# A transformer layer on one core: two attention output banks, one bank for queries and keys, value projection biases moved to the output bias, and an order of its own at both ends

## The chip, the core and the metric

The kernel runs on one core of one Trainium2 chip. The core's engines work side by side and meet through semaphores: TensorE (PE, with its weight loads as PEld), VectorE (DVE), ScalarE (ACT), GpSimd (POOL) and SyncE (SP), which issues the transfers. The metric is the device time of one execution in microseconds, less is better.

## What is computed

32 sequences of 256 tokens and 128 features go through attention (16 heads of 64) and a feed-forward part with low-rank experts, each behind a layer norm and with a layer norm on its output before the residual is added:

```python
def _L0_attn_ref(x, W_Q, b_Q, W_K, b_K, W_V, b_V, W_O, b_O):
    Q = jnp.einsum('btd,hkd->bthk', x, W_Q) + b_Q
    K = jnp.einsum('btd,hkd->bthk', x, W_K) + b_K
    V = jnp.einsum('btd,hkd->bthk', x, W_V) + b_V
    scores = jnp.einsum('bqhk,bshk->bhqs', Q, K) / jnp.sqrt(jnp.asarray(d_head, x.dtype))
    attn = jax.nn.softmax(scores, axis=-1)
    out_h = jnp.einsum('bhqs,bshk->bqhk', attn, V)
    return jnp.einsum('bqhk,hdk->bqd', out_h, W_O) + b_O
...
    gate = jax.nn.softmax(xt @ gate_w.T, axis=-1)
    base = xt @ weight.T
    t = jnp.einsum('nh,erh->ner', xt, lora_U)
    lora = jnp.einsum('ne,eor,ner->no', gate, lora_V, t)
    out = base + scaling * lora
...
    x = x + _layernorm(_L0_attn_ref(_layernorm(x, axis=-1), ...), axis=-1)
    x = x + _layernorm(_L0_ffn_ref(_layernorm(x, axis=-1), ...), axis=-1)
```

## The kernel before

One item is one sequence b (0 to 31). Heads are handled two at a time, as pairs p = 0 to 7. Projections, scores and output projection are made of three matmuls each on values split into an upper and a lower half (`_hi`, `_lo`, type fp32r); transpositions and the attention output run on fp32.

An item goes through these steps; each is a function with the engine's name above it in the code:

- `stats_x` (VectorE), `ln_rstd`, `norm_x` (GpSimd): layer norm of x. `transpose_xn` (TensorE), `xt_high` (ScalarE), `xt_low` (VectorE): transposed into `xt_hi` and `xt_lo`, plus one. The kernel adds one to x and takes it back through the weights: at the start each weight is centred so that the bias rides on it (`diagonals` on GpSimd, `weight_means` on TensorE, `fold_means` on VectorE, then `weight_hi` on ScalarE and `weight_lo` on VectorE).
- `project_qk(b,p)` (TensorE, six matmuls of 256 columns), `qk_hi` (ScalarE), `qk_lo` (VectorE).
- `project_v(b,quarter)`, three matmuls of 512 columns, `copy_v` (ScalarE).
- `scores(b,p)`, 24 matmuls of 64 rows, two at a time, into `st_ps[p % 2]`; `row_max(b,p,h)` (VectorE), `exponentials` (ScalarE), `invert_sum` (VectorE), `scale_probs` (GpSimd), for each head h of the pair.
- `transpose_probs(b,p,h)` back into the same bank, four transpositions; `copy_probs_t` (h = 0 ScalarE, h = 1 VectorE).
- `probs_v(b,p)`: attention output, eight matmuls of 64 columns of weights, two pairs to a bank; `attention_hi` (ScalarE) and `attention_lo` (VectorE) for each group of two pairs.
- `output_projection` (24 matmuls), `copy_yt`, `transpose_y`, `stats_y`, `residual_x1`, `transpose_x1`, `copy_x1t`, `project_tg`, `gate_max`, `gate_exponentials`, `apply_gate`, `transpose_u`, `copy_ut`, `project_z`, `copy_z`, `stats_z`, `norm_z`: the rest, all through the one bank `extra_ps`. The result is written over the item's x and sent out.

Each engine has its own list of these calls, written out by hand in `body(i)`, which serves three items at once: the first half of item i, the second half of i - 1, the feed-forward part of i - 2. The lists set the order; nothing is reordered on the way. `run` unrolls `body` for i = 0, 1, 2, loops over i = 3 to 31 (29 passes), and unrolls it twice more; in the unrolled ones `live` drops the calls of items that don't exist.

The eight banks of the matmul results are four for scores (`st_ps`), two for queries and keys (`qk_ps`, by p % 2), one for attention output (`o_ps`) and `extra_ps`. A call's `free=` names the semaphore that says that the bank's last content has been read.

Of the kernel before, what the change touches and what calls it, by code (L numbers as in the profile page):

```python
# [13 lines left out]
P = 128  # L14
# [11 lines left out]


# [8 lines left out]


def live(i, lag):

    return not isinstance(i, int) or 0 <= i - lag < B  # L40


def latest(i, *uses):

    for lag, sem, count in uses:
        if live(i, lag):
            return sem, count
    return uses[0][1], 0
# [6 lines left out]
def transformer_layer(nc, x, w_q, w_k, w_v, w_o, biases, ffn_w, out):  # L55
    ctx = ExitStack()
    with ctx:
# [21 lines left out]
        one = sb("one", [P, 1])  # L79
        w_o_mean = sb("w_o_mean", [P, PAIRS])  # L80
# [37 lines left out]
        qk_ps = [bank(f"qk_ps{n}") for n in range(2)]  # L118
        o_ps = bank("o_ps")
# [12 lines left out]
        diag_ready = {n: sem(f"diag_ready_{n}") for n in "qkv"}  # L132
# [9 lines left out]
        ffn_means_projected = sem("ffn_means_projected")  # L142
        w_hi_ready = {n: sem(f"w_hi_ready_{n}") for n in "qkvo"}
# [58 lines left out]
        def x_tile(b, j):  # L202
# [9 lines left out]
            ("v", slice(0, 512), st_ps[1][0], slice(0, 512)),  # L212
            ("v", slice(512, 1024), st_ps[1][1], slice(0, 512)),
            ("q", slice(256, 512), o_ps, slice(0, 256)),
            ("q", slice(512, 1024), st_ps[0][0], slice(0, 512)),
            ("k", slice(256, 512), st_ps[1][0], slice(0, 256)),
            ("k", slice(512, 1024), st_ps[0][1], slice(0, 512)),
# [3 lines left out]
        diag_home = {"v": 1, "q": 2, "k": 3}  # L221
# [45 lines left out]
        def _(pe):  # L267
            def transpose_tiles(dst, src):
# [4 lines left out]
            def weight_means(n, cols, bank, dst):  # L273

                nc.tensor.matmul(bank[:, dst], mean_w[:, :], diag(n, cols),
# [4 lines left out]
            def transpose_xn(b, free):  # L280
                after(pe, *free)
                pe.wait_ge(xn_ready, b + 1)
                transpose_tiles(extra_ps, xn).then_inc(x_transposed, 1)
                if first(b):
                    for n in "qk":
                        pe.wait_ge(diag_ready[n], 1)
                        pe.wait_ge(early_loaded[n], 16)
                    for piece in MEANS[0:2]:
                        weight_means(*piece)

            def project_qk(b, p, free):
# [8 lines left out]
                after(pe, *free)  # L300
# [7 lines left out]
                if first(b) and p == 0:  # L308
                    pe.wait_ge(diag_ready["v"], 2)
                    pe.wait_ge(w_loaded["v"], 16)  # L310
                    for piece in MEANS[2:4]:
                        weight_means(*piece)
                if first(b) and p == 1:
                    pe.wait_ge(mean_folded, 4)
                    for n, pieces in (("q", MEANS[4:6]), ("k", MEANS[6:8])):
                        pe.wait_ge(diag_ready[n], 3)
                        pe.wait_ge(w_loaded[n], 16)
                        for piece in pieces:
                            weight_means(*piece)
                if first(b) and p == 3:  # L320
                    pe.wait_ge(mean_folded, len(MEANS))
                    pe.wait_ge(ffn_rows_centred, 1)
# [800 lines left out]
```

## Time and profile before

| | |
|---|---|
| Median of three runs | 1220.18 us (1218.62 to 1221.35) |
| Profiled execution | 1221.85 us, span 1220.0 us |
| Mean granted TensorE clock | 0.990 |
| TensorE busy | 1185.9 us (97%) |
| ScalarE busy | 967.9 us (79%) |
| VectorE busy | 958.6 us (79%) |
| GpSimd busy | 728.3 us (60%) |

The span runs from the first to the last instruction; the profiled execution took 1.85 us more than its span. Busy is the time in which an engine has an instruction under way. For TensorE the ends of matmuls are modelled and overlap, so its pace is read from the distance between starts.

### The profile page before, as it was taken

Reading aid. Unit: us, or ns where it says so; the run is one execution under the profiler, and the core shown is the slowest. Engines: PE = TensorE matmul, PEld = TensorE weight load, DVE = VectorE, ACT = ScalarE, POOL = GpSimd, SP = SyncE. Lnnn points to the kernel's source line nnn. Section 1 sums busy time; section 2 is a strip of 40 time slices with the busy share of each in tenths; the row PEclk is TensorE's granted clock in tenths of the full one; section 3 lists DMA queues with packets and bytes.
Section 4 is the critical chain, followed back from the end, with each engine's and each line's share of the span. In section 5 each row is a group of like instructions: output and inputs, shape, how many; then the busy total and the mean of one; then the engine's idle time right before and its main releaser. Section 6 shows DMA issues by size and latency. Waiting matters only on the chain.

```text
span 1220.0 us, 32981 instructions
## 1 busy us (share of the span) xinstructions
PE 1185.9 (97%) x10532; PEld 977.1 (80%) x10532; DVE 958.6 (79%) x2618; ACT 967.9 (79%) x3079; POOL 728.3 (60%) x946
## 2 busy tenths in 40 slices
PE   6899999999999999999999999999999999999995
PEld 3688888888888888888888888888888888888883
DVE  4677888887888887887877878877888878788883
ACT  2678888888888888888888888888888888888882
POOL 2556556665556665566665666675556665555653
PEclk9899999999999999999999999999999999999997
DMA  6000000000000000000000000000000000000000
GB/s 213 2 1 6 2 6 4 4 4 4 0 4 4 4 4 4 0 4 4 4 4 4 4 0 4 4 4 4 4 0 4 4 4 4 4 0 4 4 4 9
DMA packets 9923, 10.95 MB, mean 9 GB/s; under 512 B 816, under 2 KB 9392, under 8 KB 9904
## 3 DMA queue, kind: packets, MB, share of 16 engines
q1 hardware_dynamic: 9904, 10.70, 2.7%
q8 instruction: 11, 0.18, 0.1%
q14 instruction: 8, 0.07, 0.0%
HBM read 6.50 MB, written 4.19 MB: 9 GB/s over the span
## 4 chain that ended last, share of the span: by engine, by line
PE 82%; POOL 7%; DVE 6%; issue 4%; ACT 1%; POOLq 0%; DVEq 0%; DMA 0%; SPq 0%; ACTq 0%
PE o_ps L383 17%; PE st_ps L365 17%; PE st_ps L355 14%; PE extra_ps L398 8%; PE qk_ps L304 4%; PE qk_ps L306 4%; PE qk_ps L305 4%; POOL probs L1021 3%; PE extra_ps L337 3%; PE extra_ps L339 2%; PE extra_ps L338 2%; DVE probs_t L806 2%; PE extra_ps L270 2%; POOL xn L1010 1%; POOL xn L1015 1%
## 5 line engine op out<-in xcount | busy, mean ns | idle before, releaser
L1021 POOL TENSOR_TENSOR probs<-probs,inv_sum 128x512 f32<-128x512 f32 x512 | 525.4, 1042 | 352.6 <-DVE inv_sum L801 342.0
L563 ACT ACTIVATE probs<-st_ps,neg_max 128x256 f32<-128x256 f32 x1024 | 475.2, 482 | 102.6 <-DVE neg_max L794 99.7
L794 DVE TENSOR_REDUCE neg_max<-st_ps 128x2 f32<-128x512 f32 x512 | 332.0, 680 | 48.8 <-PE st_ps L355 45.7
L365 PE MATMUL st_ps<-ident,probs 128*128 128x128 f32 x2048 | 286.6, 275 | 6.7 <-POOL probs L1021 5.1
L365 PEld LDWEIGHTS st_ps<-ident,probs 128*128 128x128 f32 x2048 | 233.9, 141 | 46.9 <-POOL probs L1021 21.6
L383 PE MATMUL o_ps<-probs_t,v_sb 128*64 128x256 f32 x2048 | 256.3, 387 | 0.3 <-DVE o_lo L812 0.2
L563 ACT ACTIVATION_READ_ACCUMULATOR probs<-st_ps,neg_max 128x1 f32 x1024 | 217.1, 212 | 0.0
L806 DVE COPY probs_t<-st_ps 128x512 f32<-128x512 f32 x256 | 169.4, 683 | 37.4 <-PE st_ps L365 37.3
L383 PEld LDWEIGHTS o_ps<-probs_t,v_sb 128*64 128x64 f32 x2048 | 133.4, 136 | 73.2 <-issue 5.9
L778 DVE TENSOR_TENSOR qk_lo<-qk_ps,qk_hi 128x512 fp32r<-128x512 f32 x256 | 175.1, 684 | 11.8 <-ACT qk_hi L550 11.5
L571 ACT COPY probs_t<-st_ps 128x512 f32<-128x512 f32 x256 | 152.5, 596 | 32.6 <-PE st_ps L365 32.6
L550 ACT CAST qk_hi<-qk_ps 128x512 fp32r<-128x512 f32 x256 | 152.6, 596 | 17.7 <-PE qk_ps L306 13.8
L355 PE MATMUL st_ps<-qk_hi 64*128 64x256 f32 x1024 | 165.2, 316 | 0.2 <-DVE probs_t L806 0.2
L801 DVE RECIPROCAL inv_sum<-row_sum 128x2 f32<-128x2 f32 x512 | 80.3, 162 | 92.5 <-ACT probs L563 84.1
L355 PE MATMUL st_ps<-qk_lo,qk_hi 64*128 64x256 f32 x1024 | 146.7, 279 | 0.0
L355 PE MATMUL st_ps<-qk_hi,qk_lo 64*128 64x256 f32 x1024 | 145.9, 277 | 0.0
L355 PEld LDWEIGHTS st_ps<-qk_hi 64*128 64x128 f32 x1024 | 98.6, 185 | 24.6 <-issue 17.0
L355 PEld LDWEIGHTS st_ps<-qk_lo,qk_hi 64*128 64x128 f32 x1024 | 99.6, 187 | 0.0
L355 PEld LDWEIGHTS st_ps<-qk_hi,qk_lo 64*128 64x128 f32 x1024 | 99.2, 186 | 0.0
L583 ACT COPY v_sb<-extra_ps 128x512 f32<-128x512 f32 x128 | 76.0, 594 | 29.0 <-PE extra_ps L339 29.0
L304 PE MATMUL qk_ps<-xt_hi,wq_hi 128*128 128x256 f32 x256 | 92.4, 361 | 4.5 <-issue 2.5
L989 POOL TENSOR_TENSOR rstd<-var_eps,neg_half 128x2 f32<-128x2 f32 x128 | 88.8, 694 | 10.0
(116 smaller groups left out, 2073.4 us busy)
## 6 DMA issues: line engine op xcount, KB each, us to landing
out<-x_all SPq DMA_DIRECT2D x32, 128.0 KB, 1.7
x_all<-in_x SPq DMA_DIRECT2D x1, 3840.0 KB, 17.3
stage_v<-in_w_v SPq DMA_DIRECT2D x1, 512.0 KB, 4.1
stage_o<-in_w_o SPq DMA_DIRECT2D x1, 512.0 KB, 6.7
stage_q<-in_w_q SPq DMA_DIRECT2D x1, 384.0 KB, 4.7
stage_k<-in_w_k SPq DMA_DIRECT2D x1, 384.0 KB, 5.8
x_all<-in_x SPq DMA_DIRECT2D x2, 128.0 KB, 3.1
ffn<-in_ffn_w SPq DMA_DIRECT2D x1, 196.0 KB, 6.8
```

The lines of the kernel that those rows point to most:

```text
L304: nc.tensor.matmul(dst, w_hi[w][:, cols], xt_hi[:, :], start=True, stop=False)
L355: last = nc.tensor.matmul(st_ps[p % 2][h][:, j * T:(j + 1) * T], tile(q, j)[head_rows(h), :], k[head_rows(h), :], start=(t == 0), stop=(t ...
L365: last = nc.tensor.transpose(st_ps[p % 2][h][:, s * T + j * P:s * T + (j + 1) * P], probs[p % N_PROBS][h][:, j, s * P:(s + 1) * P], ident[ ...
L383: last = nc.tensor.matmul(o_ps[head_rows(h), cols], v_sb[:, s, p * P + h * DH:p * P + (h + 1) * DH], probs_t[p % N_PROBS_T][h][:, s, :], s ...
L398: last = nc.tensor.matmul(extra_ps[:, 0:T], w["o"][:, cols], o[:, pair, :], start=(pair == 0 and n == 0), stop=(pair == PAIRS - 1 and n == 2))
L550: nc.scalar.copy(qk_hi_sb[p % N_QK][:, :], qk_ps[p % 2][:, :]).then_inc(qk_hi_ready, 1)
L563: last = nc.scalar.activation(probs[n][h][:, j, :], st_ps[p % 2][h][:, j * T:(j + 1) * T], ACT.Exp, bias=neg_max[n][h][:, j:j + 1], accum_ ...
L571: nc.scalar.copy(probs_t[p % N_PROBS_T][0][:, :, :].rearrange("p s q -> p (s q)"), st_ps[p % 2][0][:, :]).then_inc(probs_t_copied[0], 1)
L778: nc.vector.tensor_tensor(qk_lo_sb[n][:, :], qk_ps[p % 2][:, :], f32(qk_hi_sb[n][:, :]), ALU.subtract).then_inc(qk_lo_ready, 1)
L794: nc.vector.tensor_reduce(neg_max[p % N_PROBS][h][:, :], st_ps[p % 2][h][:, :].rearrange("p (j s) -> p j s", j=NT), AX.X, ALU.max, negate= ...
L806: nc.vector.tensor_copy(probs_t[p % N_PROBS_T][1][:, :, :].rearrange("p s q -> p (s q)"), st_ps[p % 2][1][:, :]).then_inc(probs_t_copied[1 ...
L1021: nc.gpsimd.tensor_tensor(probs[n][h][:, :, :], probs[n][h][:, :, :], inv_sum[n][h][:, :].unsqueeze(2).to_broadcast([P, NT, T]), ALU.mult) ...
```

## The change

Five things change.

1. **Banks.** `o_ps` becomes two banks, chosen by the group (`p // 2 % 2`). The output projection goes into `o_ps[1]` instead of `extra_ps`. In exchange `qk_ps` becomes one bank, so that each `project_qk` waits for the `qk_lo` of the pair before it (before: of the pair two before).
2. **Values.** The value weights are no longer centred and biased. The softmax weights of a row sum to one, so what is left out is a constant; it is computed once (`ffn_means`, `centre_ffn_columns`) and added to the output bias (`output_bias`, `centre_output_bias`).
3. **Order in the loop.** All five lists are new. Attention output of pairs 0 to 3 stands in a row, each pair's scores stand alone.
4. **Order at the ends.** Items 0 to 2 and what follows item 31 have lists of their own, written out call by call, instead of `body` with dropped calls.
5. **Warm-up.** Twelve 128-column matmuls on constants stand first on TensorE, and ScalarE's first instruction is a copy of `one`.

```diff
+WARM_UPS = 12
...
-        qk_ps = [bank(f"qk_ps{n}") for n in range(2)]
-        o_ps = bank("o_ps")
+        qk_ps = bank("qk_ps")
+        o_ps = [bank(f"o_ps{n}") for n in range(2)]
...
-            for i in range(lag + 1):
-                body(i)
             with engine.Fori(0, B - 1 - lag) as step:
                 body(step + (lag + 1))
-            for i in range(B, B + lag):
-                body(i)
...
+            def warm_up():
+
+                for _ in range(WARM_UPS):
+                    nc.tensor.matmul(st_ps[1][1][:, 0:P], mean_w[:, :], mean_w[:, :], start=True, stop=True)
...
+            def output_bias():
+
+                pe.wait_ge(v_offset_ready, 1)
+                pe.wait_ge(ffn_ready, 1)
+                pe.wait_ge(w_o_centred, 1)
+                dst = o_ps[1][:, D + TG + PAIRS:D + TG + PAIRS + 1]
+                nc.tensor.matmul(dst, neg_mean_w[:, :], bias[:, B_O:B_O + 1], start=True, stop=False)
+                for pair in range(PAIRS):
+                    last = nc.tensor.matmul(dst, stage["o"][:, pair_cols(pair)], v_offset[:, pair:pair + 1],
+                                            start=False, stop=(pair == PAIRS - 1))
+                last.then_inc(bias_o_projected, 1)
...
-                    dst = qk_ps[p % 2][:, n * T:(n + 1) * T]
+                    dst = qk_ps[:, n * T:(n + 1) * T]
...
+            weight_means(3)
+            project_qk(0, 0)
+            weight_means(4)
+            project_v(0, 1, free=(v_copied[0], 1))
+            weight_means(5)
+            project_qk(0, 1, free=(qk_lo_ready, 1))
+            ffn_means()
+            project_v(0, 2, free=(v_copied[1], 1))
+            scores(0, 0)
+            scores(0, 1)
+            project_qk(0, 2, free=(qk_lo_ready, 2))
+            output_bias()
...
+                scores(i, 4, free0=(probs_t_copied[0], PAIRS * i + 3), free1=(probs_t_copied[1], PAIRS * i + 3))
+                transpose_y(i - 1, free=(v_copied[3], i + 1))
+                project_qk(i, 6, free=(qk_lo_ready, PAIRS * i + 6))
+                scores(i, 5, free0=(probs_t_copied[0], PAIRS * i + 4), free1=(probs_t_copied[1], PAIRS * i + 4))
+                probs_v(i, 0, free=(o_lo_ready, GROUPS * i - 1))
+                probs_v(i, 1)
+                probs_v(i, 2, free=(yt_ready, i))
+                probs_v(i, 3)
+                project_qk(i, 7, free=(qk_lo_ready, PAIRS * i + 7))
+                transpose_x1(i - 1, free=(x1_ready, i))
+                transpose_probs(i, 4, 1, free=(exp_ready[1], PAIRS * i + 5))
+                transpose_probs(i, 4, 0, free=(exp_ready[0], PAIRS * i + 5))
+                transpose_probs(i, 5, 1, free=(exp_ready[1], PAIRS * i + 6))
```

**The loop, scores of pairs 4 and 5 on TensorE.** Before, the two pairs' scores follow one another and attention output of pair 1 follows them (`st_ps` are scores, `o_ps` is attention output, `yt` is the transposition of the output, `qk_ps` a projection):

```order
L270 MATMUL extra_ps<-ident,yt 128x128 x2
L343 REGISTER_ALU
L355 MATMUL st_ps<-qk_hi 128x256 x2
...
L355 MATMUL st_ps<-qk_hi,qk_lo 128x256 x2
L343 REGISTER_ALU
L355 MATMUL st_ps<-qk_hi 128x256 x2
...
L355 MATMUL st_ps<-qk_hi,qk_lo 128x256 x2
L383 MATMUL o_ps<-probs_t,v_sb 64x256 x4
L304 MATMUL qk_ps<-xt_hi,wq_hi 128x256
```

The same place of the changed kernel:

```order
L370 MATMUL st_ps<-ident,probs 128x128 x4
L360 MATMUL st_ps<-qk_hi 128x256 x2
...
L360 MATMUL st_ps<-qk_hi,qk_lo 128x256 x2
L263 MATMUL extra_ps<-ident,yt 128x128 x2
L259 REGISTER_ALU
L326 MATMUL qk_ps<-xt_hi,wq_hi 128x256
...
L328 MATMUL qk_ps<-xt_hi,wk_lo 128x256
L360 MATMUL st_ps<-qk_hi 128x256 x2
...
L360 MATMUL st_ps<-qk_hi,qk_lo 128x256 x2
L259 REGISTER_ALU
L387 MATMUL o_ps<-probs_t,v_sb 64x256 x16
```

The transposition of yt and projection 6 have moved between the two pairs' scores, and the attention output behind them is of four pairs.

**The loop, attention output of pairs 6 and 7.** On TensorE of the changed kernel the scores of item i's pair 0, the last transpositions of item i - 1, projection 2 and the attention output follow one another:

```order
L360 MATMUL st_ps<-qk_hi,qk_lo 128x256 x2
L370 MATMUL st_ps<-ident,probs 128x128 x4
L259 REGISTER_ALU
L326 MATMUL qk_ps<-xt_hi,wq_hi 128x256
...
L328 MATMUL qk_ps<-xt_hi,wk_lo 128x256
L259 REGISTER_ALU
L387 MATMUL o_ps<-probs_t,v_sb 64x256 x8
L360 MATMUL st_ps<-qk_hi 128x256 x2
```

Before, the scores of pair 0 were followed by the transposition of u, transpositions of probabilities, projection 3, `project_z`, the scores of pair 1, and then this attention output. VectorE of the changed kernel has at that place, with the maximum of pair 0 (`neg_max`) ahead of the copy of pair 7 (`probs_t`):

```order
L1084 TENSOR_REDUCE gate_max_raw<-extra_ps 128x2
L1089 TENSOR_TENSOR gate_neg_max<-gate_max_raw,rstd 128x2
L1035 REGISTER_ALU
L1037 TENSOR_TENSOR qk_lo<-qk_ps,qk_hi 128x512
L1042 TENSOR_REDUCE neg_max<-st_ps 128x2
L1054 COPY probs_t<-st_ps 128x512
L1042 TENSOR_REDUCE neg_max<-st_ps 128x2
```

Before, one maximum of pair 0 stood ahead of that copy as well, but with more of TensorE's work between.

**The start, VectorE.** Before, from the fold of the last early piece to the first maximum:

```order
L704 TENSOR_TENSOR stage_k<-stage_k,st_ps 128x512
L694 SCALAR_TENSOR_TENSOR wq_lo<-stage_q,wq_hi 128x768
L778 TENSOR_TENSOR qk_lo<-qk_ps,qk_hi 128x512
L694 SCALAR_TENSOR_TENSOR wk_lo<-stage_k,wk_hi 128x768
L746 TENSOR_REDUCE w_o_mean<-stage_o 128x8
L749 TENSOR_SCALAR w_o_mean<-w_o_mean 128x8
L794 TENSOR_REDUCE neg_max<-st_ps 128x2
```

After, from the statistics of item 2 (`stats_x(2)`, the rows that read `x_all`) on:

```order
L967 BN_STATS stats<-x_all 128x6 x2
L970 COPY stats_seen<-stats 128x1
L972 BN_AGGR mean_var<-stats 128x2 x2
L961 TENSOR_TENSOR stage_k<-stage_k,o_ps 128x256
L1037 TENSOR_TENSOR qk_lo<-qk_ps,qk_hi 128x512
L952 SCALAR_TENSOR_TENSOR wq_lo<-stage_q,wq_hi 128x768
L952 SCALAR_TENSOR_TENSOR wo_lo<-stage_o,wo_hi 128x1024
L961 TENSOR_TENSOR stage_k<-stage_k,st_ps 128x512
L1037 TENSOR_TENSOR qk_lo<-qk_ps,qk_hi 128x512
L1022 TENSOR_TENSOR v_offset<-bias,o_ps 128x8
L1025 TENSOR_TENSOR ffn<-ffn,o_ps 128x264
L952 SCALAR_TENSOR_TENSOR wk_lo<-stage_k,wk_hi 128x768
```

The statistics of items 1 and 2 have moved ahead of the first `qk_lo`, and the set-up of the output weights and the feed-forward weights ahead of the first maximum, which is the next instruction. Items 2 to 31 come in one transfer, the last that SyncE issues before its loop.

## Rows read from the trace of the kernel before

**Rows 1.** The page, its groups by cost: busy us, mean ns of one

```profile
PE 1185.9 (97%) x10532; PEld 977.1 (80%) x10532; DVE 958.6 (79%) x2618; ACT 967.9 (79%) x3079; POOL 728.3 (60%) x946
...
L806 DVE COPY probs_t<-st_ps 128x512 f32<-128x512 f32 x256 | 169.4, 683 | 37.4 <-PE st_ps L365 37.3
```

**Rows 2.** Windows: stretch, its us, busy us (instructions) by engine

```profile
core 0: us, PE busy (x) PEld busy (x) DVE busy (x) ACT busy (x) POOL busy (x), PEclk, DMA share, GB/s
...
20.00:30.00 10.00, 7.46 (x29) 4.70 (x28) 7.55 (x12) 4.17 (x6) 0.00 (x0) 1.00 0.20 64
30.00:40.00 10.00, 7.83 (x55) 6.32 (x55) 6.39 (x18) 7.39 (x22) 5.03 (x4) 0.83 0.01 2
40.00:50.00 10.00, 7.02 (x54) 5.11 (x54) 6.53 (x19) 5.34 (x20) 4.99 (x5) 0.92 0.00 1
...
600.00:700.00 100.00, 99.86 (x903) 82.24 (x901) 81.64 (x220) 83.51 (x268) 60.57 (x78) 1.00 0.01 3
```

**Rows 3.** The tile xn on TensorE, whole span, and 91 to 94 us

```profile
L270 PE MATMUL extra_ps<-ident,xn x64: 272/273/445, 7.5 to 1147.5; 128*128 128x128 f32 x64
...
L270 PE MATMUL extra_ps<-ident,xn x2: 272/272/273, 92.5 to 92.6; 128*128 128x128 f32 x2
```

**Rows 4.** TensorE's timeline, 679 to 690 us: start, us, what

```profile
679.82 0.28 PE L306 MATMUL qk_ps<-xt_hi,wk_lo 128*128 128x256 f32 x1
680.03 0.39 PE L355 MATMUL st_ps<-qk_hi 64*128 64x256 f32 x2
680.25 0.28 PE L355 MATMUL st_ps<-qk_lo,qk_hi 64*128 64x256 f32 x2
680.37 0.28 PE L355 MATMUL st_ps<-qk_hi,qk_lo 64*128 64x256 f32 x2
...
683.53 0.50 PE L337 MATMUL extra_ps<-wv_hi,xt_hi 128*128 128x512 f32 x1
683.87 0.39 PE L338 MATMUL extra_ps<-wv_lo,xt_hi 128*128 128x512 f32 x1
684.10 0.40 PE L339 MATMUL extra_ps<-wv_hi,xt_lo 128*128 128x512 f32 x1
...
688.32 0.60 PE L365 MATMUL st_ps<-ident,probs 128*128 128x128 f32 x4
688.68 0.36 PE L304 MATMUL qk_ps<-xt_hi,wq_hi 128*128 128x256 f32 x1
...
689.47 0.38 PE L433 MATMUL extra_ps<-ffn,x1t 128*128 128x128 f32 x2
```

**Rows 5.** Timelines of TensorE and GpSimd, 709 to 711 us

```profile
709.18 3.20 POOL L1021 TENSOR_TENSOR probs<-probs,inv_sum 128x512 f32<-128x512 f32 x3
...
709.95 0.28 PE L306 MATMUL qk_ps<-xt_hi,wk_lo 128*128 128x256 f32 x1
...
710.28 0.66 PE L365 MATMUL st_ps<-ident,probs 128*128 128x128 f32 x4
```

**Rows 6.** Timeline of all engines, 26 to 39 us

```profile
26.30 0.95 DVE L694 SCALAR_TENSOR_TENSOR wq_lo<-stage_q,wq_hi 128x768 fp32r<-128x768 f32 x1
...
31.10 0.28 PE L355 MATMUL st_ps<-qk_hi,qk_lo 64*128 64x256 f32 x2
...
31.42 0.69 DVE L794 TENSOR_REDUCE neg_max<-st_ps 128x2 f32<-128x512 f32 x1 [1.38 <-PE st_ps L355]
...
38.27 1.84 PE L365 MATMUL st_ps<-ident,probs 128*128 128x128 f32 x12 [0.40 <-POOL probs L1021]
```

**Rows 7.** SyncE's timeline at 5 us, and transfers: KB, us to landing

```profile
5.61 0.61 SPq L259 DMA_DIRECT2D x_all<-in_x  x1
...
x_all<-in_x SPq DMA_DIRECT2D x1, 3840.0 KB, 17.3
```

**Rows 8.** Timeline of all engines, 1198 to 1200 us

```profile
1198.75 0.39 PE L398 MATMUL extra_ps<-o_hi,wo_hi 128*128 128x256 f32 x1
1198.87 0.59 ACT L576 CAST o_hi<-o_ps 128x512 fp32r<-128x512 f32 x1 [1.51 <-PE o_ps L383]
...
1199.49 0.69 DVE L812 TENSOR_TENSOR o_lo<-o_ps,o_hi 128x512 fp32r<-128x512 f32 x1 [1.27 <-ACT o_hi L576]
```

More of the change, by code:

```diff
@@ new lines, in _ @@
+            invert_sum(0, 0, 1)
+            invert_sum(0, 1, 0)
+            invert_sum(0, 1, 1)
+            copy_probs_t(0, 0)
+            qk_lo(0, 3)
+            row_max(0, 2, 0)
+            row_max(0, 2, 1)
+            copy_probs_t(0, 1)
+            invert_sum(0, 2, 0)
+            qk_lo(0, 4)
+            stats_x(3)
+            invert_sum(0, 2, 1)
+            attention_lo(0, 0)
+            row_max(0, 3, 1)
+            row_max(0, 3, 0)
+            qk_lo(0, 5)
+            copy_probs_t(0, 2)
@@ new lines, in _ @@
+            invert_sum(0, 3, 1)
+            invert_sum(0, 3, 0)
+            qk_lo(0, 6)
+            row_max(0, 4, 0)
+            copy_probs_t(0, 3)
+            row_max(0, 4, 1)
+            invert_sum(0, 4, 0)
+            invert_sum(0, 4, 1)
+            row_max(0, 5, 1)
+            row_max(0, 5, 0)
+            qk_lo(0, 7)
+            xt_low(1)
+            copy_probs_t(0, 4)
+            invert_sum(0, 5, 1)
+            invert_sum(0, 5, 0)
+            attention_lo(0, 1)
+            qk_lo(1, 0)
@@ new lines, in _ @@
+            invert_sum(1, 0, 1)
+            qk_lo(1, 3)
+            attention_lo(0, 3)
+            row_max(1, 1, 0)
+            row_max(1, 1, 1)
+            copy_probs_t(1, 0)
+            invert_sum(1, 1, 0)
+            invert_sum(1, 1, 1)
+            qk_lo(1, 4)
+            copy_probs_t(1, 1)
+            qk_lo(1, 5)
+            row_max(1, 2, 0)
+            row_max(1, 2, 1)
+            row_max(1, 3, 1)
+            invert_sum(1, 2, 0)
+            row_max(1, 3, 0)
+            stats_y(0)
@@ new lines, in _ @@
+            invert_sum(1, 2, 1)
+            invert_sum(1, 3, 1)
+            residual_x1(0)
+            invert_sum(1, 3, 0)
+            stats_x1(0)
+            qk_lo(1, 6)
+            copy_probs_t(1, 2)
+            copy_probs_t(1, 3)
+            copy_x1t(0)
+            attention_lo(1, 0)
+            qk_lo(1, 7)
+            row_max(1, 4, 0)
+            row_max(1, 4, 1)
+            row_max(1, 5, 1)
+            invert_sum(1, 4, 0)
+            row_max(1, 5, 0)
+            xt_low(2)
+            invert_sum(1, 4, 1)
@@ new lines, in _ @@
+            stats_z(0)
+            qk_lo(2, 5)
+            row_max(2, 2, 0)
+            row_max(2, 2, 1)
+            row_max(2, 3, 1)
+            invert_sum(2, 2, 0)
+            row_max(2, 3, 0)
+            invert_sum(2, 2, 1)
+            invert_sum(2, 3, 1)
+            invert_sum(2, 3, 0)
+            copy_probs_t(2, 2)
+            copy_probs_t(2, 3)
+            stats_y(1)
+            row_max(2, 4, 0)
+            row_max(2, 4, 1)
+            qk_lo(2, 6)
+            invert_sum(2, 4, 0)
@@ new lines, in _ @@
+            residual_x1(1)
+            attention_lo(2, 0)
+            row_max(2, 5, 1)
+            row_max(2, 5, 0)
+            invert_sum(2, 4, 1)
+            stats_x1(1)
+            invert_sum(2, 5, 1)
+            copy_x1t(1)
+            qk_lo(2, 7)
+            invert_sum(2, 5, 0)
+            copy_probs_t(2, 4)
+            attention_lo(2, 1)
+            copy_probs_t(2, 5)
+            xt_low(3)
+            row_max(2, 6, 0)
+            row_max(2, 6, 1)
+            row_max(2, 7, 0)
@@ new lines, in _ @@
+            invert_sum(2, 6, 0)
+            row_max(2, 7, 1)
+            invert_sum(2, 6, 1)
+            qk_lo(3, 0)
+            gate_max(1)
+            invert_sum(2, 7, 0)
+            invert_sum(2, 7, 1)
+            copy_probs_t(2, 6)
+            qk_lo(3, 1)
+            row_max(3, 0, 0)
+            copy_probs_t(2, 7)
+            apply_gate(1)
+            row_max(3, 0, 1)
+            qk_lo(3, 2)
+            invert_sum(3, 0, 0)
+            row_max(3, 1, 0)
+            invert_sum(3, 0, 1)
```

1203 lines of the change are left out of this document (800 added, 403 removed).

## The prediction

> **What bounds the kernel now.** I read the page's first lines, then the windows, the waits of TensorE, and the timeline of one steady item. TensorE is busy for 97% of the span [rows 1]. In the steady middle it is busy 99.86 of 100 us at the full clock, with VectorE at 82, ScalarE at 84 and GpSimd at 61 [rows 2]. Item starts (the transposition of xn) lie at 92.6 and 1147.5 for items 2 and 31, so one item takes (1147.5 - 92.6) / 29 = 36.38 us [rows 3]. Thirty-two items are 1164 us of 1220; some 56 us lie at the ends. So only two things can move the time: what TensorE needs per item (29 passes of the loop), and the ends. An engine with slack, or a bank that comes free earlier, is worth nothing in the loop unless TensorE waits for it. It waits in one real place: `transpose_probs(i,4,0)` starts 0.33 us after the matmul before it where 0.12 is the pace, on the end of GpSimd's scaling (709.18 plus one third of 3.20 us, against 710.28) [rows 5]. That is 0.21 us per pass, 6 us in all.
>
> **What TensorE pays per item now.** The matmuls of both kernels are the same in number and shape in the loop; only their order and banks change. But the timeline shows that order has a price. TensorE runs three array shapes: 128\*128 (projections, transpositions), 64\*128 (scores), 128\*64 (attention output). Within a shape a start follows the last by 0.12 us (680.25 to 680.37 for a pair of score matmuls). At a change of shape the last of the old takes 0.21 (679.82 to 680.03) and the first of the new 0.22 (680.03 to 680.25), or 0.34 instead of 0.23 for a 512-column one after attention output (683.53, 683.87, 684.10) [rows 4]. So one change of shape costs about 0.09 + 0.10 = 0.19 us. Going from a transposition to a projection costs nothing of the kind (688.32 to 688.68 is 0.36 for four transpositions, to 689.47 is 0.79 for six projection matmuls, together 1.15 for ten) [rows 4].
>
> The Trainium skill says so too, and it speaks against this change: TensorEngine Tiling (Array Packing), section Key Properties, has it that changing the tiling mode, not merely the tile, drains TensorE. It gives no price; the rows above agree with it.
>
> **The loop's order, counted.** I counted stretches of one shape in the order of both kernels. Before, a pass has five stretches of scores (pairs 6 and 7 together, 0, 1, 2 and 3 together, 4 and 5 together), five of attention output, six of the rest: 16 changes. After, all eight scores stand alone, attention output has three stretches (4-5, 6-7, 0 to 3), the rest eight: 19 changes. "Four pairs in a row" saves two stretches and the split scores add three, each with a stretch of the rest beside it. That is 3 x 0.19 = +0.57 us per pass. The wait on GpSimd should go: the two transpositions of pair 4 now stand behind attention output of four pairs (about 3.6 us) and projection 7, while GpSimd's input for it does not come later; -0.21. Net +0.36 per pass, x 29 = **+10.4 us**. Outside the loop the two orders differ by 99 - 87 = 12 further changes, **+2.3 us**.
>
> **One bank for queries and keys.** `project_qk(p+1)` now waits for `qk_lo(p)`. Its path is 0.3 to start (as 31.10 to 31.42) [rows 6], 0.6 on ScalarE, 0.7 on VectorE (as the two copies of a bank at the end) [rows 8]. That is 1.6 us. The narrowest place of the new order is between projections 1 and 2: two sets of transpositions (0.36 each), scores (0.8) and a change of shape on either side, 1.9 us from last matmul to first [rows 4]; between the others lie 2 to 7 us. I walked one pass with these durations and found the answer 0.2 us early there and 0.4 or more elsewhere. I take 0, and up to 0.3 per pass as upper bound. Two attention banks: before, attention output waited nowhere in the loop for its bank, so the second saves nothing there; I take 0, also as a lower bound.
>
> **A new wait.** The hand walk found one. Attention output of pairs 6-7 needs `copy_probs_t(7)` on VectorE, and in VectorE's order `row_max(i,0,0)` stands ahead of that copy. That maximum starts 0.32 us after the last score row (31.10 to 31.42) [rows 6], the next instruction 0.62 later, the copy takes 0.68 [rows 1], hand-over 0.06 (710.22 to 710.28) [rows 5]: 1.68. TensorE has between that score row and the attention output 0.21, one set of transpositions 0.36, projection 2 at 0.79 and 0.09 for leaving the shape: 1.45 [rows 4]. So it waits 0.23; behind it stand scores of pair 1 and all that follows. Before, three blocks lay in that place. Bounds 0 and 0.4; I take 0.2, **+5.8 us**.
>
> **The start.** Now: first maximum at 31.42, first transposition of probabilities at 38.27 [rows 6]; TensorE is busy 7.5, 7.8 and 7.0 us of the stretches 20 to 30, 30 to 40 and 40 to 50, at clocks 1.00, 0.83 and 0.92 [rows 2]. The change drops the folding of means into the value weights (four of the 512-column pieces on TensorE, two on VectorE), brings the table load and the weights' upper halves forward, and warms TensorE up. But VectorE now meets `stats_x(2)` ahead of `qk_lo(0,0)`, and its input is the 3840 KB transfer, issued at 5.61 and landing 17.3 us later, at 22.9 [rows 7]. All of VectorE's work behind it waits, and so does projection 1 on TensorE, which stays idle from about 16 to 25. From 22.9 on stand statistics, folds, `qk_lo` twice, two small centrings, and lower halves of 768, 1024 and 768 columns. The last three are 0.95 for 768 [rows 6] and four thirds of it for 1024, 3.2; the two `qk_lo` 1.4 (as a copy of a bank) [rows 1]; for the rest, eight short operations on smaller tiles, I estimate 3 from the same rate. The first maximum comes at about 30 to 32, no earlier than now by more than 1.5. What follows is better ordered: no set-up of VectorE is left between the first maxima, so the first transposition comes at about 35 and scores of pair 5 some 5 us earlier than now, with attention output further on. I take **-8 us**, bounds -3 (TensorE at half clock after its pause) and -12 (no gap at all behind the first transposition).
>
> **The end.** Output projection now accumulates in the second attention bank, which also holds the last group. Before, 18 of its 24 matmuls ran while that group was still being copied (1198.75 on, ScalarE 1198.87, VectorE 1199.49) [rows 8]; now the first waits for both copies, 1.3 us and hand-overs. Waits of the last pairs shrink a little. **+1 us**, bounds 0 and +2. In the loop the same wait for `o_lo` is covered: transpositions, a value projection, projection 3.
>
> **Sum:** 10.4 + 2.3 + 5.8 - 8 + 1 = +11.5. The profiled execution took 1221.85 (span 1220.0 and 1.85 around it), the median of the runs is 1220.18, 1.67 lower: 1231.7, so 1232.
>
> **The rivals.**
> A, the forecast: changes of shape decide, with the small new wait; 1226 to 1241. Chance 0.52.
> B: no new wait, and a start better than I take: 10.4 + 2.3 - 11 + 1 = +2.7, 1223; range 1218 to 1226. For it speaks that a hand walk rounds against the kernel; against it, VectorE standing until 22.9. Chance 0.19; about half of it is within 0.2%.
> C, the other side: faster, because a change of shape is cheaper where the new stretches are short (scores to projection and attention output to scores hardly occur in the loop now, so no steady row prices them). At half the price a pass has 0.28 - 0.21 = +0.07, 2 us; outside 1.1; with -8 + 1 that is -4, 1216; at no price -13, 1207. It decides below 0.13 us per change (5 us from the ends over 29 passes, plus the 0.21 that goes). Against it: both ends of every change in the steady rows cost 0.09 or more. Chance 0.13.
> D: more waits. ScalarE and VectorE are 82% busy and the walk left 0.4 us at several places (scores of 0, 2, 3); if three of them miss by 0.15, +13 more: 1245. The longest ranges of slack in the order before were longer, since pairs of scores bought time. Chance 0.16.
>
> **Numbers.** 0.2% (2.4 us) is about what a measurement of this kernel can tell from no change. Faster by more than that is C alone and a little of B: 0.14. Within it, most of the lower half of B: 0.09. Slower: 0.77. The range leaves out C and the end of D: 1219 to 1244.
>
> **What would show it.** Right: item period 36.9 to 37.1 between transpositions of xn; 0.2 us at each change of shape, also for scores to projection; no wait of `transpose_probs(4,0)` on GpSimd, and one of about 0.2 before attention output of pair 6 on VectorE's copy; VectorE idle until 22.9 on the x transfer; first transposition of probabilities near 35. Wrong: a period at or below 36.5 (then C), or above 37.3 with waits for `probs_t` or `qk_lo` spread over the pass (D), or a steady state reached 10 us earlier than now (B).

## The result, and the profile after

The changed kernel takes 1236.24 us (median of 4 runs, 1235.91 to 1236.63), the kernel before 1220.13 on the same chip: ratio 1.0133, 95% interval 1.0115 to 1.0150. It is slower, by less than 2%. The forecast was 1232 with a range of 1219 to 1244. The profiled execution has a span of 1234.4 us against 1220.0.

The page's first line and the windows of the kernel after (stretch, its us, busy us of each engine, granted clock) answer to [rows 1, 2]:

```profile
PE 1203.6 (98%) x10580; PEld 999.8 (81%) x10580; DVE 970.8 (79%) x2617; ACT 953.9 (77%) x3080; POOL 724.4 (59%) x944
```

```profile
core 0: us, PE busy (x) PEld busy (x) DVE busy (x) ACT busy (x) POOL busy (x), PEclk, DMA share, GB/s
20.00:30.00 10.00, 6.21 (x27) 5.89 (x27) 5.32 (x13) 1.43 (x2) 0.88 (x2) 0.61 0.15 51
30.00:40.00 10.00, 10.00 (x68) 8.75 (x66) 4.84 (x12) 5.29 (x19) 3.06 (x4) 0.70 0.00 1
40.00:50.00 10.00, 8.97 (x77) 6.84 (x76) 8.30 (x20) 7.50 (x25) 5.66 (x9) 1.00 0.01 2
600.00:700.00 100.00, 100.00 (x900) 82.89 (x899) 82.48 (x229) 80.76 (x263) 63.35 (x84) 1.00 0.01 4
```

TensorE is now busy for all of the middle, and still the kernel is slower: it gets through the same matmuls of a pass more slowly. From 20 to 40 us its granted clock is 0.61 and 0.70, where it was 1.00 and 0.83.

The transpositions of xn on TensorE in the kernel after, over the whole span and near 136 us, answer to [rows 3]:

```profile
L263 PE MATMUL extra_ps<-ident,xn x64: 272/273/328, 7.2 to 1161.6; 128*128 128x128 f32 x64
...
L263 PE MATMUL extra_ps<-ident,xn x2: 273/273/273, 136.2 to 136.3; 128*128 128x128 f32 x2
```

Item 3 is the first whose transposition stands at the same place of the work in both lists. It starts at 136.2 (before 128.8), that of item 31 at 1161.5 (before 1147.3), and the span ends 72.9 us later (before 72.7). So the 14.4 us are +7.4 up to item 3, +6.8 over 28 items (0.24 each, of which the first pass, with 37.58, has 1.2 us alone; behind it a pass takes 36.58 against 36.38), and +0.2 at the end. By then four pairs' attention output "in a row" has done 1.9 us and transpositions another 0.7 that were still to come before; counted in work, the start is some 4.8 and the end some 2.8 longer.

Where the 0.20 us of a steady pass come from shows when TensorE's time is summed by kind (each block from its first start to the first start of the next, my sum over the trace, mean of 27 passes, the first pass of the loop left out):

```
us per pass                         before   after   pair 4   projection  scores pulled
                                                     moved    1 between   forward
scores                               6.75     7.28      6.75       6.94       7.14
attention output                     7.66     7.36      7.66       7.66       7.36
projections of queries and keys      6.58     6.68      6.43       6.60       6.67
gate projection                      0.46     0.57      0.46       0.46       0.57
values, output projection, z         7.06     7.06      7.07       7.08       7.06
all transpositions                   7.87     7.65      7.90       8.51       7.65
sum                                 36.38    36.58     36.26      37.25      36.44
```

(The last three columns are experiments below.) Three more stretches of scores cost 0.53, two fewer of attention output give back 0.30, and the rest falls on the blocks between.

The table leaves half of each change of shape with the neighbouring block. Summed at the changes themselves (the last step from start to start in the old shape and the first in the new, less the pace inside the shape; over 20 passes of the trace), the 16 changes of a pass cost 2.92 us before and the 19 cost 3.58 after. That is 0.18 and 0.19 each, and every kind of change lies between 0.15 and 0.23. So three more changes cost 0.65, and 0.45 went elsewhere. Most of it went at the end of a pass. TensorE there, before (projection 7, transposition of pair 4, jump back, transposition of xn, attention output):

```profile
564.46 0.28 PE L306 MATMUL qk_ps<-xt_hi,wk_lo 128*128 128x256 f32 x1
564.78 0.66 PE L365 MATMUL st_ps<-ident,probs 128*128 128x128 f32 x4
565.34 0.43 PE L270 MATMUL extra_ps<-ident,xn 128*128 128x128 f32 x2
565.70 0.87 PE L383 MATMUL o_ps<-probs_t,v_sb 128*64 128x256 f32 x6
```

and after (twelve transpositions of probabilities, jump back, transposition of xn):

```profile
574.89 1.47 PE L370 MATMUL st_ps<-ident,probs 128*128 128x128 f32 x12
576.20 0.38 PE L263 MATMUL extra_ps<-ident,xn 128*128 128x128 f32 x2
576.42 0.60 PE L370 MATMUL st_ps<-ident,probs 128*128 128x128 f32 x4
```

After, each transposition takes 0.11 (1.31 for twelve, 0.22 for the two of xn). Before, the step to the transposition of pair 4 took 0.32, 0.21 more than the pace, its four took 0.56 instead of 0.44, and the two of xn 0.36, which is 0.05 more than 0.22 and a change's 0.09. These 0.38 us have gone; another 0.08 went at the scores of pair 3 (0.89 before where the second pair of a couple takes 0.81), whose cause I have not looked into.

### The profile page after: what moved, and what is told of

Read it like the earlier page. It is cut to its first block, busy times and chain, and to the rows that moved or that the text cites. A ratio compares the mean times of both kernels' runs of the same rounds, so it can differ in the third digit from the quotient of the medians.

```text
span 1234.4 us, 33065 instructions
## 1 busy us (share of the span) xinstructions
PE 1203.6 (98%) x10580; PEld 999.8 (81%) x10580; DVE 970.8 (79%) x2617; ACT 953.9 (77%) x3080; POOL 724.4 (59%) x944
## 4 chain that ended last, share of the span: by engine, by line
PE 94%; DVE 2%; DMA 1%; POOL 1%; ACT 1%; issue 0%; SPq 0%; POOLq 0%; DVEq 0%; ACTq 0%
PE o_ps L387 19%; PE st_ps L360 19%; PE st_ps L370 18%; PE o_ps L401 8%; PE qk_ps L326 6%; PE qk_ps L328 5%; PE qk_ps L327 5%; PE extra_ps L263 3%; PE extra_ps L340 3%; PE extra_ps L342 2%; PE extra_ps L341 2%; PE extra_ps L423 2%; DMA x_all<-in_x 1%; PE extra_ps L436 1%; PE extra_ps L438 1%; POOL probs L1497 1%
## 5 line engine op out<-in xcount | busy, mean ns | idle before, releaser
L1042 DVE TENSOR_REDUCE neg_max<-st_ps 128x2 f32<-128x512 f32 x512 | 341.1, 681 | 90.6 <-PE st_ps L360 85.8
L387 PE MATMUL o_ps<-probs_t,v_sb 128*64 128x256 f32 x2048 | 244.4, 385 | 0.2 <-ACT probs_t L710 0.2
L702 ACT ACTIVATION_READ_ACCUMULATOR probs<-st_ps,neg_max 128x1 f32 x1024 | 220.5, 215 | 0.0
L387 PEld LDWEIGHTS o_ps<-probs_t,v_sb 128*64 128x64 f32 x2048 | 138.7, 137 | 73.5 <-issue 1.8
L1054 DVE COPY probs_t<-st_ps 128x512 f32<-128x512 f32 x256 | 175.1, 685 | 14.1 <-PE st_ps L370 10.5
L360 PE MATMUL st_ps<-qk_hi 64*128 64x256 f32 x1024 | 171.2, 330 | 1.5 <-ACT probs_t L710 1.3
```

The lines of the kernel that those rows point to most:

```text
L360: last = nc.tensor.matmul(st_ps[p % 2][h][:, j * T:(j + 1) * T], tile(q, j)[head_rows(h), :], k[head_rows(h), :], start=(t == 0), stop=(t ...
L387: last = nc.tensor.matmul(o_ps[p // 2 % 2][head_rows(h), cols], v_sb[:, s, p * P + h * DH:p * P + (h + 1) * DH], probs_t[p % N_PROBS_T][h] ...
L702: last = nc.scalar.activation(probs[n][h][:, j, :], st_ps[p % 2][h][:, j * T:(j + 1) * T], ACT.Exp, bias=neg_max[n][h][:, j:j + 1], accum_ ...
L1042: nc.vector.tensor_reduce(neg_max[p % N_PROBS][h][:, :], st_ps[p % 2][h][:, :].rearrange("p (j s) -> p j s", j=NT), AX.X, ALU.max, negate= ...
L1054: nc.vector.tensor_copy(probs_t[p % N_PROBS_T][1][:, :, :].rearrange("p s q -> p (s q)"), st_ps[p % 2][1][:, :]).then_inc(probs_t_copied[1 ...
```

## The experiments

In the code cuts the arguments are left out. Each ratio is to the kernel before, run on the same chip; chips differ from experiment to experiment.

**A change of shape, by itself.**

```diff
-project_qk(i, 1, ...)
 scores(i - 1, 6, ...)
+project_qk(i, 1, ...)
 scores(i - 1, 7, ...)
```

> The kernel before, with projection 1 of the next item put between the scores of pairs 6 and 7, which stood in a row; nothing else is changed. A pass gets two changes of array shape more, with the same matmuls. If a change of shape costs TensorE 0.19 us wherever it stands, the period grows by 0.38 us and 30 items by some 11 to 12 us (1232 against 1220). If short stretches change shape more cheaply, or the cost is hidden, the time stays within 3 us of before.

1248.58 us, ratio 1.0228 (1.0211 to 1.0244): more than either theory said. TensorE's waits from 150 to 1150 us (waited for: us in total, times, longest), and its timeline at one of them:

```profile
PE st_ps L355 <- DVE probs_t L807: 10.9, 27, 0.4
```

```profile
618.58 1.04 PE L365 MATMUL st_ps<-ident,probs 128*128 128x128 f32 x8
...
620.02 0.39 PE L355 MATMUL st_ps<-qk_hi 64*128 64x256 f32 x2 [0.40 <-DVE probs_t L807]
```

Of 0.87 us more per pass, 0.47 is a new wait (from 618.58 to 620.02 it is 1.44, where eight transpositions and a change take 0.97): scores of pair 6 now come before VectorE has copied the transpositions that stood in their bank; projection 1 had covered that copy. The other 0.40 belong to two changes. The table shows the scores apart at 6.94 instead of 6.75, which is half of it. A change of shape does cost 0.20 here; and a block that is moved also stops covering what it covered.

**The wait on GpSimd, by itself.**

```diff
-transpose_probs(i, 4, 0, ...)        # end of the pass
 ...
 probs_v(i - 1, 3)
+transpose_probs(i - 1, 4, 0, ...)
 transpose_probs(i - 1, 4, 1, ...)
```

> The kernel before, with the first transpositions of pair 4 moved from the end of a pass to the next pass, directly ahead of the second ones. It takes away TensorE's wait for GpSimd's scaling and nothing else; the number of changes of shape is the same. If the wait is worth only what I read (0.21 us), the period falls by 0.2 and the time by 6 us. If the jump back to the head of the loop had been paid for too, because nothing was queued in front of TensorE when it waited, the period falls by 0.33 to 0.38 and the time by 9 to 11. If GpSimd only makes another instruction late instead, it falls by nothing.

1217.80 us, ratio 0.9976 (0.9965 to 0.9988), period 36.26 instead of 36.38. The projections of queries and keys fall by 0.15 and the transpositions of probabilities by another 0.12: 0.27 at a place where I had read 0.21, and the last step before the jump back still takes 0.17 where 0.12 is the pace. But the transposition of xn grows by 0.16, up to a wait of TensorE's weight load (150 to 1150 us):

```profile
PEld o_ps L383 <- DVE o_lo L812: 9.1, 28, 0.3
```

Attention output of pair 2 now meets its one bank before VectorE has read it. The wait on GpSimd had hidden this one. In the changed kernel, with its second bank, there is no such row; its order differs too, so the bank by itself is not shown to be the reason.

**Joining scores again, three ways.** First all four, by pulling projections ahead:

```diff
 transpose_probs(i - 1, 5, 0, ...)
-scores(i - 1, 6, ...)
 project_qk(i, 0, ...)
+scores(i - 1, 6, ...)
 scores(i - 1, 7, ...)
...
-scores(i, 4, ...)
 transpose_y(i - 1, ...)
 project_qk(i, 6, ...)
+scores(i, 4, ...)
 scores(i, 5, ...)
```

> The changed kernel, with scores of pairs 4 and 5 and of pairs 6 and 7 put in a row again in the loop (projection 6 with the transposition of y goes ahead of scores 4, projection 0 ahead of scores 6). A pass has four changes of shape fewer, 15. If they cost 0.19 us each and no wait comes in their place, the period falls by 0.76 us, and the time by 22 us, to some 1214, below the kernel before. If the other engines' order makes TensorE wait for the banks of scores or of queries and keys, part of that is lost: 1220 to 1236. If changes of shape are free, nothing moves.

1298.87 us, ratio 1.0643 (1.0629 to 1.0658). It has four changes of shape fewer and is 5% slower than the change itself. TensorE's waits, 150 to 1150 us:

```profile
PE qk_ps L326 <- DVE xt_lo L992: 21.8, 26, 0.8
PE st_ps L370 <- POOL probs L1497: 6.7, 25, 0.3
PE extra_ps L263 <- ACT v_sb L722: 6.2, 26, 0.2
```

Projection 0 stands right behind the transposition of xn and waits 0.8 for its two halves, and scores that come later make GpSimd's scaling late. These idle times are 1.3 us of the 2.3 by which a pass grew; the rest I have not traced. Then only pairs 4 and 5, on the kernel with the late statistics (below, 1225.31):

```diff
-scores(i, 4, ...)
-transpose_y(i - 1, ...)
 project_qk(i, 6, ...)
+transpose_y(i - 1, ...)
+scores(i, 4, ...)
 scores(i, 5, ...)
```

> The changed kernel with the late statistics (1225.3), and in the loop projection 6 and the transposition of y ahead of the scores of pair 4 instead of behind them: scores of pairs 4 and 5 in a row, 17 changes of shape instead of 19. Between the last quarter of values and the transposition of y stand a set of transpositions and projection 6 (1.15 us), so the wait on the copy of values seen when all four scores were joined should not come. Scores of pair 4 start 1.2 us later; from their end to the transposition of pair 4 there are still 5.5 us. If only changes of shape count: period -0.38, time -11, some 1214. If the chain of pair 4 (maximum, exponentials, scaling) is longer than 5.5 us, its transpositions wait and half or more of it is lost: 1219 to 1226.

1234.30 us, ratio 1.0113 (1.0096 to 1.0130), and 0.26 us more per pass. The timeline of GpSimd and TensorE at the head of the loop:

```profile
602.15 3.04 POOL L1497 TENSOR_TENSOR probs<-probs,inv_sum 128x512 f32<-128x512 f32 x3 [0.40 <-DVE inv_sum L1049]
...
604.80 0.43 PE L263 MATMUL extra_ps<-ident,xn 128*128 128x128 f32 x2
...
605.33 0.65 PE L370 MATMUL st_ps<-ident,probs 128*128 128x128 f32 x4
```

The scaling of pair 5 ends at 605.19, and its transposition starts at 605.33, 0.53 after that of xn where 0.22 is the pace: not pair 4 but the end of the same chain is late. Last, the second of each couple pulled forward, on the same kernel:

```diff
 scores(i, 4, ...)
+scores(i, 5, ...)
 transpose_y(i - 1, ...)
 project_qk(i, 6, ...)
-scores(i, 5, ...)
...
 scores(i - 1, 6, ...)
-project_qk(i, 0, ...)
 scores(i - 1, 7, ...)
+project_qk(i, 0, ...)
```

> The changed kernel with the late statistics (1225.3), with the same two pairs of scores joined as in the run that joined all four, but by pulling the second of each forward (pair 5 directly behind pair 4, pair 7 directly behind pair 6) instead of putting projections ahead of the first. No score comes later than now. A pass has 17 changes of shape, two fewer. If a change costs 0.19 us here too and what spoiled the joined versions was only the lateness of their scores: period -0.38, time -11, some 1214. If the copies of the transpositions just ahead are late for the pulled scores, waits of 0.1 to 0.2 appear there: 1217 to 1221. If changes of shape in this order cost nothing, 1225.

1221.28 us, ratio 1.0000 (0.9990 to 1.0009): 4 us faster than without, not 11. The period falls by 0.14. TensorE and ScalarE where pair 7 follows pair 6:

```profile
601.75 0.58 ACT L710 COPY probs_t<-st_ps 128x512 f32<-128x512 f32 x1
```

```profile
602.26 0.28 PE L360 MATMUL st_ps<-qk_hi,qk_lo 64*128 64x256 f32 x2
602.43 0.38 PE L360 MATMUL st_ps<-qk_hi 64*128 64x256 f32 x2
602.62 0.31 PE L360 MATMUL st_ps<-qk_lo,qk_hi 64*128 64x256 f32 x2
```

Pair 7 starts 0.17 after pair 6's last matmul instead of 0.12, just behind the copy's end (602.33), and the next follows 0.19 later instead of 0.12. So this joined pair gives back 0.12 of its 0.19; over the pass, two changes fewer kept 0.14 us.

**Attention output in a row, in the kernel before.**

```diff
 scores(i, 3, ...)
-probs_v(i, 0, ...)
 output_projection(i - 1, 0, ...)
...
 scores(i, 5, ...)
+probs_v(i, 0, ...)
 probs_v(i, 1)
```

(on the kernel with the transpositions of pair 4 moved, 1217.80)

> The kernel before with the first transpositions of pair 4 moved (1217.8), and attention output of pair 0 moved down beside that of pair 1, behind the scores of pairs 4 and 5. It is one part of the change (attention output in a row) by itself; 15 changes of shape instead of 16, and no other engine's order moves. If a change costs 0.19 us: period -0.19, time -6, some 1212. If attention output of pair 0 had covered a copy that now is waited for, less than half of it.

1238.06 us, ratio 1.0139 (1.0124 to 1.0155). TensorE's waits, 150 to 1150 us:

```profile
PE st_ps L365 <- POOL probs L1021: 9.8, 27, 0.4
```

Attention output falls from 7.66 to 7.51 as it should. But the transpositions of pair 2, which come 1.0 us earlier after their scores, wait for GpSimd: with all that follows the period grows by 0.63, to 36.89. I had looked for a copy that it covered, and the cover was for the softmax chain.

**The statistics at the start.**

```diff
 fold_means(3)
-stats_x(2)
 fold_means(4)
 qk_lo(0, 0)
 ...
 weight_lo("k", late, ...)
+stats_x(2)
 row_max(0, 0, 0)
```

> The changed kernel, with the statistics of the whole x transfer moved on VectorE from ahead of the first lower half of queries and keys to just ahead of the first maximum of scores. VectorE stood idle there from 17.6 to 22.0 us on the transfer. If that wait is what spoiled the start, the first maximum comes 3 to 4.4 us earlier and the time falls by 3 to 5 us. If what follows is set by something else (TensorE at half clock, its one-column matmuls, the waits in the hand-written lists of items 1 and 2), the first maximum may come earlier and the time moves by less than 1.5 us.

1225.31 us, ratio 1.0044 (1.0030 to 1.0058): 10.9 us less, more than twice what I allowed. In the kernel after, VectorE and TensorE wait one for the other, and then:

```profile
22.02 0.49 DVE L967 BATCH_NORM_STATS2 stats<-x_all 128x6 f32<-128x128 f32 x2 [4.45 <-DMA x_all<-in_x]
...
23.81 0.58 PE L326 MATMUL qk_ps<-xt_hi,wq_hi 128*128 128x256 f32 x1 [3.79 <-DVE qk_lo L1037]
...
26.14 3.41 PE L291 MATMUL o_ps<-one,stage_v 128*128 128x1 f32 x16
29.41 0.77 PE L340 MATMUL extra_ps<-wv_hi,xt_hi 128*128 128x512 f32 x1
...
31.35 0.41 PE L360 MATMUL st_ps<-qk_lo,qk_hi 64*128 64x256 f32 x2
31.56 0.41 PE L360 MATMUL st_ps<-qk_hi,qk_lo 64*128 64x256 f32 x2
```

The same blocks with the statistics late:

```profile
18.09 0.39 PE L326 MATMUL qk_ps<-xt_hi,wq_hi 128*128 128x256 f32 x1 [0.21 <-DVE qk_lo L1037]
...
19.34 1.84 PE L291 MATMUL o_ps<-one,stage_v 128*128 128x1 f32 x16
21.05 0.48 PE L340 MATMUL extra_ps<-wv_hi,xt_hi 128*128 128x512 f32 x1
...
22.14 0.28 PE L360 MATMUL st_ps<-qk_lo,qk_hi 64*128 64x256 f32 x2
22.25 0.28 PE L360 MATMUL st_ps<-qk_hi,qk_lo 64*128 64x256 f32 x2
```

After the pause TensorE starts a pair of score matmuls every 0.21 us instead of every 0.12, and this lasts until 35: the lower of its two levels, 1.2 of 2.4 GHz (the granted clock is 0.50 in each 2 us stretch from 24 to 34). In this run item 3 begins at 125.0, 3.8 us before the kernel before, with its 2.6 us more work done.

**The pause filled, the wait kept.**

```diff
 weight_means(5)
+for _ in range(20):
+    nc.tensor.matmul(o_ps[0][:, :], tile(xt_hi, 0), w_hi["v"][:, 0:HALF], start=True, stop=True)
 project_qk(0, 1, ...)
```

> The changed kernel as it was measured, with 20 matmuls more whose result nobody reads (values of item 0 once more, into the free first attention bank), put into TensorE's idle time ahead of the second projection at the start. VectorE's wait for the x transfer stays. If the wait alone made the start slow, the time stays at 1236 or grows a little. If TensorE's pause of 5 us cost a second time, through the half clock that followed it (from 24 to 35 us), the blocks behind it get their full-clock times (4.15 to 2.15 us for the means, 2.86 to 1.62 for the first scores, and four more): 5 to 5.5 us less, some 1231, although TensorE does more.

1230.14 us, ratio 1.0080 (1.0065 to 1.0095): 6.1 us less than the change, with 4.6 us more for TensorE to do. The granted clock is 1.00 from 18 to 40 us, the means take 2.15 us and the first scores 1.62. So of the 11 us that the statistics cost, some 6 are the half clock and some 5 the wait.

**The output bias, and the tail**, both on the kernel with the late statistics:

```diff
-output_bias()
 project_v(0, 3, ...)
 transpose_probs(0, 0, 0, ...)
 project_qk(0, 3, ...)
+output_bias()
```

(VectorE's `centre_output_bias` moves behind three inverses to match.)

> The changed kernel with the late statistics (1225.3), and the nine one-column matmuls of the output bias moved from ahead of the first transposition of probabilities to behind projection 3, where TensorE waited for GpSimd's scaling. If they only lay in the way of the first transposition, it comes 1.9 us earlier and the wait behind it is filled: 0.7 to 1.9 us less. If GpSimd's scaling sets the first transposition, nothing changes.

1227.88 us, ratio 1.0064 (1.0044 to 1.0083), against 1.0044 (1.0030 to 1.0058) without. The median is 2.6 higher and the profiled run 5, but the intervals overlap: there is no gain, and a loss is not certain. The first transposition comes at 27.61 instead of 27.07, set by GpSimd's scaling, as the second theory had it; the values ahead of it are done early and TensorE is idle for 1.2 us there. Behind the one-column matmuls its clock then falls:

```profile
20.00:30.00 10.00, 8.81 (x79) 7.72 (x77) 8.08 (x21) 7.30 (x24) 4.03 (x6) 1.00 0.12 41
30.00:40.00 10.00, 9.98 (x68) 8.42 (x68) 4.94 (x15) 4.48 (x13) 3.25 (x5) 0.66 0.00 0
```

```diff
 scores(31, 6, ...)
-probs_v(31, 4, ...)
-probs_v(31, 5)
 scores(31, 7, ...)
+probs_v(31, 4, ...)
+probs_v(31, 5)
```

(ScalarE's list is changed to match.)

> The changed kernel with the late statistics (1225.3), and at the very end the scores of pair 7 directly behind those of pair 6, ahead of attention output of pairs 4 and 5, with ScalarE's order to match. If the tail of the change is longer because the last pair's scores come late (and not because the output projection shares the second attention bank), the end comes 1 to 2 us earlier: 1223.5 to 1224.5. If the bank sets it, nothing changes.

1226.19 us, ratio 1.0049 (1.0032 to 1.0067), no gain. From the last transposition of xn to the first matmul of the output projection it is 50.2 us, against 49.9. Pair 7's scores come nearly 2 us earlier, but the last inverse of its sums, whose exponentials end at 1194, starts at 1195.70: on VectorE it stands behind the gate's maximum. That the output projection waits for its bank is there (0.32 us, on o_lo), but small. What sets the tail I have not isolated.

**A better order for the kernel before.** With the transpositions of pair 4 moved, on ScalarE:

```diff
 exponentials(i, 4, 0)
-exponentials(i, 4, 1)
 attention_hi(i, 0)
+exponentials(i, 4, 1)
```

> The kernel before with the first transpositions of pair 4 moved (1217.8), and on ScalarE the copy of the first attention output group ahead of the second exponentials of pair 4. There TensorE no longer waits for GpSimd, but attention output of pair 2 waits 0.16 us for the lower half of that group, which the wait on GpSimd had hidden before. If it is that bank, the wait goes: period -0.16, time -4.5, some 1213. If the exponentials come too late for the transpositions of pair 4 instead, nothing is won.

1235.00 us, ratio 1.0116 (1.0097 to 1.0135). TensorE's waits:

```profile
PE extra_ps L270 <- DVE x1t L864: 10.7, 27, 0.4
```

On VectorE the inverse of pair 4's sums waits for the later exponentials, and the copy of x1 behind it for nothing but its turn. So:

```diff
-invert_sum(i - 1, 4, 1)
 copy_x1t(i - 2)
 attention_lo(i - 1, 0)
+invert_sum(i - 1, 4, 1)
```

> The last kernel, and on VectorE the inverse of the second row sums of pair 4 moved behind the copy of x1 transposed and the lower half of the first attention output group. The last kernel lost 0.5 us a pass because that inverse waited for the delayed exponentials, and the copy of x1 (for which the transposition of xn waits) stood behind it. If that was all, the 0.5 us go, and the wait for the attention bank (0.16) as well: some 1213 against 1217.8 for the first transpositions of pair 4 moved alone. If ScalarE's delay of 0.6 us reaches pair 5 or the projections, there are waits there: 1218 or more.

1218.36 us, ratio 0.9975 (0.9963 to 0.9988). The 0.5 us are gone, but the bank's wait stays: VectorE's lower half starts right behind the copy of x1 (561.78, 562.12), wherever ScalarE's copy is. It is the same as moving the transpositions alone. These two are the fastest here, 0.25% below the kernel before.

## Why the prediction was right, and where it was not

The sum said +11.5 us. The spans of the profiled runs differ by 14.4, and the medians by 16.1, because the profiled run of the kernel before was 1.7 above its median and that of the changed kernel was not. That the forecast is only 4 us low is partly luck, since two of its parts failed in opposite directions: the loop got +16.2 and took +6.8, the start got -8 (and part of 2.3 for changes of shape) and took +7.4. Without the second, the time would have been that of the kernel with the late statistics, 1225, on the edge of rival B.

- **What bounds the kernel.** Right: TensorE per item, and the ends. Nothing else moved the time.
- **Changes of shape, +0.57 per pass.** Right: the three cost 0.65 together, 0.19 each on average (and 0.20 in the experiment with projection 1 between). Rival C (a lower price where stretches are short) is ruled out: scores to projection cost 0.20 to 0.23 and attention output to scores 0.21, and one block of scores alone takes 0.90 to 0.94 where two together take 1.61 to 1.70. The Trainium skill's rule that changing the tiling mode drains TensorE (TensorEngine Tiling (Array Packing), Key Properties) agrees with this; the price is this kernel's.
- **The wait on GpSimd, -0.21.** It went, but this term was too small. The step itself lost 0.21, as read; the transpositions behind it and the jump back lost 0.17 more, which the working had left out. With the 0.08 at pair 3's scores this, and not a lower price of a change, is why a pass grew by 0.20 and not by 0.36.
- **The new wait ahead of attention output of pairs 6-7, +5.8 us.** This step failed: the wait is not there. Timelines of the kernel after, VectorE and TensorE:

```profile
656.41 0.69 DVE L1054 COPY probs_t<-st_ps 128x512 f32<-128x512 f32 x1
...
658.14 0.28 PE L360 MATMUL st_ps<-qk_hi,qk_lo 64*128 64x256 f32 x2
...
658.46 0.69 DVE L1042 TENSOR_REDUCE neg_max<-st_ps 128x2 f32<-128x512 f32 x1
...
659.06 0.68 DVE L1054 COPY probs_t<-st_ps 128x512 f32<-128x512 f32 x1
...
659.42 0.28 PE L328 MATMUL qk_ps<-xt_hi,wk_lo 128*128 128x256 f32 x1
659.63 1.95 PE L387 MATMUL o_ps<-probs_t,v_sb 128*64 128x256 f32 x16
...
661.51 0.39 PE L360 MATMUL st_ps<-qk_hi 64*128 64x256 f32 x2
```

  The maximum does stand ahead and starts 0.32 after the score row, as I had it, and the copy behind it (659.06 to 659.74) is that of pair 7. But attention output begins with the eight matmuls of pair 6, and `probs_v(i - 1, 6)` waits only for the copies of pair 6; VectorE's began at 656.41. It starts at 659.63, 0.21 after the projection, without a wait. Pair 7's eight come 0.91 later, at 660.55, and by then their copy is done for 0.8. My own durations would have said so: the copy needs 1.68 from the score row, and TensorE reaches pair 7 after 1.45 + 0.91 = 2.36.
- **One bank for queries and keys, 0.** Right in this order: TensorE has no wait of its own from 150 to 1150 us. How much room is left I have not tested; in the joined versions the waits were for other things (above).
- **Two attention banks, 0.** Right as a sum, but the reason was too short. In the order before, the one bank made TensorE wait 0.16 as soon as the wait on GpSimd went. That the second bank is what lets the change keep that gain is likely, but the changed kernel with one bank was not run.
- **The start, -8 us.** This step failed, and not by the wait, which I had read (VectorE idle until 22.9; it was 22.0, and TensorE stood from 20 to 23.8 and not from 16 to 25). The half clock after the pause was only my bound of -3; it cost some 6 us by itself. The first maximum came at 32.66 and the first transposition at 38.28, where I had 30 to 32 and 35. Without the wait (the run with the late statistics) item 3 starts 3.8 earlier than before with 2.6 of work more done, 6.4 in all. I had taken 8, less about 2 for the eleven further changes of shape that the trace has up to there, so the rest of the term was about right.
- **The end, +1.** 0.2 in time, some 2.8 with the work already done counted, of which 1.1 is not there in the run with the late statistics. Near enough; its cause is open.
- **Own order at the ends.** The lists of items 1 and 2 leave TensorE waiting 5.1 us between 62 and 137 us, mostly for GpSimd's scaling (3.6); the row reads the same with the statistics late. I tried no other order for them.

## What to carry to other kernels

- Count stretches of one array shape when reordering matmuls on a saturated TensorE: each change here cost 0.15 to 0.23 us. But whatever is saved is kept only if the block moved was not covering a chain on other engines. Of the reorderings here that won changes of shape or removed a wait, none kept more than about half of it.
- Before pricing a wait, look at which instruction of the waiting block needs the late result. Here only the second half of the block did, and a wait of 0.2 us was in truth 0.7 us of room.
- An early wait is dear twice: a DMA that arrives 4.5 us late on one engine idled TensorE, and the half clock after it cost as much again. Put what depends on the last transfer behind everything else, or keep TensorE busy while it waits.
- Two waits in one place hide each other. Before pricing the removal of one, look at what stands just behind it.

## What the runs showed of the hardware

- TensorE's granted clock fell to half after a pause of 3.8 us at 20 us, and stayed there for 11 us of unbroken work. Matmuls whose result nobody reads kept it up. In another run it fell after one-column matmuls that followed a pause of only 1.2 us.
- Sixteen one-column matmuls took 1.84 us at full clock and 3.41 at half, about as much per matmul as 256 columns of a projection (0.12, and 0.21 at half).
- At a change of array shape TensorE took 0.15 to 0.23 us longer than at its pace, 0.18 to 0.19 on average, wherever the change stood.
- VectorE's records overlap: behind a maximum of 0.69 us (658.46) the copy starts after 0.60 (659.06).
